# Linear-attention denominators: features stationary and the block-diagonal z moving, in place of z stationary, a copy and transposes

## What is computed

```python
sq = sigma(q); sk = sigma(k)                 # sigma = elu + 1, 64 x 32
denom_q = sum(sq * z, axis=-1) + 1e-6        # z: running sum of sk over the segments before
denom_k = sum(sk * z, axis=-1) + 1e-6
A_mem  = (sq @ M) / denom_q
A      = beta * A_mem + (1 - beta) * softmax(causal(q @ k.T)) @ v
V_prev = (sk @ M) / denom_k
M      = M + sk.T @ (v - V_prev)
z      = z + sum(sk, axis=0)
```

## Time and profile before

| | |
|---|---|
| median of 3 runs | 2316.42 us (2314.68 to 2317.61) |
| profiled execution, its own time | 2315.6 us |
| its span | 2313.8 us |
| mean granted TensorE clock | 0.955 |
| PE busy | 2060.1 us (89% of the span) |
| DVE busy | 1425.9 us (62%) |
| ACT busy | 896.8 us (39%) |
| POOL busy | 389.9 us (17%) |

### The profile page before, as it was taken

One profiled execution on the slowest core, in us unless ns is written; L12 is line 12 of the kernel. 1 busy time (PEld: TensorE's weight loads), 2 busy tenths in 40 slices (PEclk: granted clock), 3 DMA queues, 4 the chain that ended last, 5 costly groups with the idle time before them and its releaser, 6 DMA issues. The chain is left out here.

```text
span 2313.8 us, 67240 instructions
## 1 busy us (share of the span) xinstructions
PE 2060.1 (89%) x29532; PEld 1685.4 (73%) x29532; DVE 1425.9 (62%) x3418; ACT 896.8 (39%) x1567; POOL 389.9 (17%) x693
## 2 busy tenths in 40 slices
PE   4999999999999999999999983188799999987994
PEld 4888888888888888888888872044477777766994
DVE  6666766766666667667666645533377777775221
ACT  3433343433343433334334330123376566654110
POOL 1222222222222222222222220300000000000011
PEclk9999999999999999999999995599899999998997
DMA  3111111111111111111111100322400000004010
GB/s 114 30 30 53 35 48 39 30 48 39 30 53 34 40 47 30 48 39 30 53 35 33 41 25 10 123 88 94 127 10 11 10 10 11 11 1 146 10 19 10
DMA packets 62819, 98.20 MB, mean 42 GB/s; under 512 B 6257, under 2 KB 26753, under 8 KB 62528
## 3 DMA queue, kind: packets, MB, share of 16 engines
q1 hardware_dynamic: 54976, 76.82, 10.8%
q0 software_dynamic: 7552, 17.07, 2.7%
HBM read 49.30 MB, written 27.26 MB: 33 GB/s over the span
## 5 line engine op out<-in xcount | busy, mean ns | idle before, releaser
L335 POOL TENSOR_TENSOR Mbd<-M,headmask 128x128 f32<-128x128 f32 x512 | 231.7, 484 | 641.7 <-DVE M L600 639.0
L1758 DVE CUSTOM_DVE_ANT_0 Sm<-Sp,mc 128x1023 f32<-128x1023 f32 x128 | 155.7, 1217 | 15.0 <-PE Sp L1800 7.6
L343 POOL TENSOR_TENSOR As<-T 128x512 f32<-128x512 f32 x64 | 93.7, 1465 | 417.6 <-DVE T L616 417.6
L1662 ACT ACTIVATE Sm<-Sm,mxs 128x1023 f32<-128x1023 f32 x128 | 147.1, 1149 | 36.9 <-DVE mxs L1760 36.7
L1828 PE MATMUL Op<-PTs,V 128*32 128x128 f32 (+1 forms) x2048 | 125.7, 276 | 0.9 <-DVE PTs L1709 0.9
L1800 PE MATMUL Sp<-KS,QS 128*128 128x512 f32 x256 | 94.6, 452 | 31.4 <-DVE mxs L1760 31.4
L1828 PEld LDWEIGHTS Op<-PTs,V 128*32 128x32 f32 (+1 forms) x2048 | 108.2, 111 | 12.1 <-issue 10.4
L590 DVE TENSOR_REDUCE mx<-S 128x16 f32<-128x1024 f32 x64 | 78.1, 1220 | 61.9 <-PE S L823 61.9
L1709 DVE COPY PTs<-Tp 128x512 f32<-128x512 f32 x128 | 88.5, 692 | 41.2 <-PE Tp L1812 41.1
L399 ACT ACTIVATE Pq<-Pq 128x1024 f32<-128x1024 f32 x64 | 68.6, 1071 | 106.9 <-DVE Pq L593 106.9
L363 ACT ACTIVATE PT<-S 128x1024 f32<-128x1024 f32 x64 | 65.6, 1026 | 114.4 <-PE S L873 114.4
(11 more groups left out here) (312 smaller groups left out, 5069.1 us busy)
## 6 DMA issues: line engine op xcount, KB each, us to landing
VS<-DV SPq DMA_DIRECT2D x64, 264.0 KB, 3.8
xin<-in_x SPq DMA_DIRECT2D x32, 512.0 KB, 4.7
out_rows<-outt SPq DMA_DIRECT2D x64, 256.0 KB, 2.0
mask_columns<-mcol SPq DMA_DIRECT2D x16, 512.0 KB, 6.5
xs<-in_w SPq DMA_DIRECT2D x16, 512.0 KB, 4.7
QT<-in_wqT SPq DMA_DIRECT2D x1, 1024.0 KB, 11.7
KT<-in_wkT SPq DMA_DIRECT2D x1, 1024.0 KB, 13.9
SQT<-in_wvT SPq DMA_DIRECT2D x1, 1024.0 KB, 16.0
```

The lines of the kernel that those rows point to most:

```text
L335: ins = pool.tensor_tensor(Mbd[:, 1 - b, g, :].rearrange("p (j d) -> p j d", j=J), bm(M[:, 1 - b, g, :], J), bc(headmask[:, :], DK), ALU.mult)
L343: pool.tensor_tensor(As[:, :], T1[:, :], T2[:, :], ALU.add).then_inc(s_as, 1)
L1662: act.activation(Sm[:, h % 4, 0:KC], Sm[:, h % 4, 0:KC], ACT.Exp, bias=mxs[:, h % 4, 1:2], accum_out=rsum[:, b, h:h + 1]).then_inc(s_e, 1)
L1758: link(dve.tensor_tensor_reduce(Sm[:, h % 4, 0:KC], Sp[h % 2][:, 0:KC], mc[:, b, 0:KC], 1.0, -3.0e38, ALU.add, ALU.max, mxs[:, h % 4, 0:1]))
```

## The change

The operands of the denominator matmuls change places. SKT or SQT, one tile of 128 tokens at a time, becomes the stationary operand (128 rows by 128 columns), and `Zbd`, now 16 columns wide, the moving one. The result has tokens on the partitions at once: for each (k or q, tile, group) 16 columns, 256 in all, in the bank of DNT. DEN is gone from both orders, and with it the copy to DT on ACT, the tile DT, and the four transposes on PE. DVE reads the same values from a bank that is packed by 16 instead of 32 columns.

```diff
-        Zbd = sb("Zbd", [P, 2, G, 32])
-        DT = sb("DT", [P, 512])
+        Zbd = sb("Zbd", [P, 2, G, SEGS * J])
...
-        ORDER = (["AST1", "OUT1", "KT0", "KT1", "V1", "SK1", "DEN", "DNT", "OUT0"],
+        ORDER = (["AST1", "OUT1", "KT0", "KT1", "V1", "SK1", "DNT", "OUT0"],
                  ["QT0", "QT1", "AST0", "V0", "SK0", "XT0", "XT1"])
-        FIRST = (["XF1", "QT1", "KT1", "V1", "SK1", "DEN", "DNT"],
+        FIRST = (["XF1", "QT1", "KT1", "V1", "SK1", "DNT"],
...
-            def den_rows(m):
-                bank, free = got(act, "DEN", m)
-                copy(DT[:, :], bank[:, :]).then_inc(free, 1)
-
...
                 if ln:
                     xT(m, "XT", 0)
-                if stage1:
-                    den_rows(m)
                 if ln:
                     xT(m, "XT", 1)
...
-            den_rows(None)
...
                 for g in range(G):
-                    ins = dve.tensor_tensor(Zbd[:, pn, g, 0:SEGS * J].rearrange("p (s j) -> p s j", j=J),
+                    ins = dve.tensor_tensor(Zbd[:, pn, g, :].rearrange("p (s j) -> p s j", j=J),
...
-                rows = bank[:, :].rearrange("p (q a g c) -> p q a g c", q=2, a=TILES, g=G)
+                rows = bank[:, 0:256].rearrange("p (q a g c) -> p q a g c", q=2, a=TILES, g=G)
...
                 pe.wait_ge(s_zbd, n + 1)
                 pe.wait_ge(s_sq, n * 2 + 2)
 
-                bank, full = take(pe, "DEN", m)
+                bank, full = take(pe, "DNT", m)
                 for q in range(2):
-                    for g in range(G):
-                        rhs = SKT[:, g, :] if q == 0 else SQT[:, pn, g, :]
-                        ins = pe.matmul(bank[32 * g:32 * g + 32, q * BT:q * BT + BT], Zbd[:, pn, g, :], rhs,
-                                        start=True, stop=True)
-                ins.then_inc(full, 1)
-
-            def den_transposes(m):
-                moved(pe, "DEN", m)
-                bank, full = take(pe, "DNT", m)
-                for c in range(4):
-                    ins = pe.transpose(bank[:, c * P:c * P + P], DT[:, c * P:c * P + P], ident[:, :])
+                    for a in range(TILES):
+                        for g in range(G):
+                            t = slice(a * P, a * P + P)
+                            o = ((q * TILES + a) * G + g) * SEGS * J
+                            ins = pe.matmul(bank[:, o:o + SEGS * J], SKT[:, g, t] if q == 0 else SQT[:, pn, g, t],
+                                            Zbd[:, pn, g, :], start=True, stop=True)
                 ins.then_inc(full, 1)
...
                 if stage1:
                     mask(m + 1, 0)
-                    den_transposes(m)
                     scores(pn, 0, 0)
...
             denominators(None, 0, 0)
-            den_transposes(None)
             x_transposes(None, 1, 1, "XT", 0)
```

## The result

The changed kernel takes 2439.66 us (median of 4 runs, 2438.95 to 2441.45) against 2315.55 us for the kernel before on the same chip: ratio 1.054, 95% interval 1.0527 to 1.0554, 124 us slower. The direction was forecast, the size was not: 2372 us was the forecast, 2360 to 2430 the range. The profiled execution took 2440.3 us, its span is 2438.6 us.

What follows compares the result with a forecast made beforehand. PE was taken to bound the attention stage, start to start. Plus 1.76 us a block x31 = 54.6, with 1.15 for the prologue, made 55.7 us: 2371.3 profiled, 2372 at the median, range 2360 to 2430.

Steps and rivals of the forecast that it cites:

- What bounds the stage: Attention stage: PE busy 1295.5 of 1300.0 us, so time between its starts counts; DVE and ACT free unless late.
- The sum of the parts: Stretch from XT0 to scores: 4.78 us against 3.02, plus 1.76 us a block, x31 = 54.6; prologue plus 1.15 us.
- The reading that fixed the price: Denominator matmuls: L1117 and L1108 show the float32 load, not the few moving columns, sets the step; 0.109 us taken.
- Rivals 2 and 3: Denominator steps: only columns count, 0.028 us, 2292, chance 0.06; load costs half, 0.054 us, 2317, chance 0.04.
- the change of tile shape and the wait for ACT: Mask ahead of DT's transposes: 0.49 us against 0.32 for the other mask, so 0.17 us removed besides the transposes' 0.56.
- Rival 4: Output projection: PE waits for DVE's late denominators beyond 0.9 us slack; 0.3 us a block gives 2381; chance 0.06.
- rival 1: Behind the denominators PE's clock falls to half once a block for 3.4 us: 53 us more, 2425; chance 0.27.

Runs made afterwards that it cites:

- the packed kernel: Kernel before, Zbd still stationary, k's and q's 16 rows of each group sharing one 32-row output, two DT transposes instead of four: 2303.48 us, ratio 0.9945.
- the four pieces: Changed kernel with its 16 denominator matmuls split into four pieces of four, placed between other work of the block: 2427.37 us, ratio 1.0478.

## Why the prediction was wrong

**What bounds the stage** held. PE was busy throughout, ACT's lost copy and DVE gave nothing, and each nanosecond between PE's starts was paid in full.

**The sum of the parts** held. At full clock the denominators take 3.57 us against 3.58, the stretch from XT0 to the scores 4.82 us in the run with 64 columns against 4.78, and that run stands at +58 us against +55.7. That 3.57 met 3.58 so closely is in part luck. The step is 0.112 us, not 0.109: (1.94 - 0.258) / 15, with 258 ns for a record by this group of the kernel after:

```profile
L791 PE MATMUL proj<-Zbd,SKT 128*128 128x16 f32 x496 | 57.7, 258 | 0.0
```

And the first of the 31 steps takes 0.03 us, which is why k's sixteen records span 1.86 us and q's 1.94. My sum had both wrong, and the two misses cancel.

The reading that fixed the price was L1117 and L1108, few columns and no shorter step. The Trainium skill, page "TensorE: Matmul & The Clock Gate", section "LDWEIGHTS (loading the stationary operand)", gives columns / 1.2 ns, an estimate of 107 ns for 128 columns. At full clock the trace, with 112 ns, is within 5% of it. Rivals 2 and 3 (0.028 and 0.054 us a step) are out by the same rows.

**One explanation within it was wrong.** Of "the change of tile shape and the wait for ACT" only the wait for ACT is left, as the packed kernel shows. The term, 0.17 us, was right.

**Rival 4** did not come true: nothing on PE waits for the denominators in the kernel after. The slack was there, and the four pieces, which used it up, paid at most 0.4 us a block for it, 6.4 us in all.

**The step that failed is the choice between the forecast and rival 1**, and then that rival's size. I gave it 0.27 because "the records lie dense, and through the steady part, dense too, the clock stayed at 1.00". That takes PE's busy share for what keeps the clock up. The kernel after is 100% busy by that share (1418.6 of 1420.0 us), and its clock falls at the denominators of every block. The run with 64 columns shows what does matter: the loads are as many and as close, more moves behind each, and the clock never fell in the steady part. I had written down myself that no row shows loads with so little behind them for so long, and then let the nearest busy rows speak for them. The size was off too: I priced one fall a block of 3.4 us at 1.7 us. The trace has 14 short stretches (period 45.38 us, 1.34 over the 44.04 at full clock) and 17 long ones (46.88, 2.84 over), 2.2 us on the mean and 67 us in all, where rival 1 had 53. In all 31 blocks this holds: where the clock falls behind the last denominator matmul (742.62, after 742.50) the stretch is short; where it falls while they still run (786.99, before 788.63) the rest of them runs at half rate as well, and the low stretch is twice as long. My range's end, 2430, allowed for one fall and a little; it was missed by 10 us. A short stretch costs 1.3 and not 1.7 us because what runs in it takes less than twice as long: from start to start T times M takes 0.55 us (0.39 in the run with 64 columns), the mask 0.54 (0.32), the scores 1.05 (0.62). Why these don't double I have not settled.

## What to carry to other kernels

Price a float32 matmul on a full tile by its two weight loads, 0.112 us each at full clock here, with 16 as with 64 moving columns; if only a few columns move, make the small operand the stationary one and let column groups work side by side, as the kernel before does. A PE that is 100% busy is not a PE at full clock: ahead of an edit that puts microseconds of loads with little moving behind them into a dense stage, price the half-rate stretches too, and look at the granted clock by window afterwards. And before exchanging the operands to save copies and transposes, look at how much of the copied tile is padding: packing two half-empty outputs into one won 13 us where the exchange lost 124.

## What I had not expected of the hardware

- More streaming, less time: 64 columns (48 of them zeros) per load took 2372.8 us and kept the clock at 1.00, 16 columns took 2439.7 us at 0.94, 32 columns 2431.4 us at 0.95.
- The same number of records of the same shape kept the clock in float32 (16 records in 1.78 us, 1.00 throughout) and lost it in eleven blocks of 31 in float32r (1.86 us). Why is open.
- A float32r matmul with its load of 128 columns takes as long, start to start, as each of float32's two records, 0.11 us.
